# Attention outputs left in their own layout, with packed softmax sums, in a macaron block

## The chip, the cores and the metric

One core of one Trainium2 chip runs the whole program. The metric is device time of one execution in microseconds (us); the kernel before took 467.0 us in the median of three runs (466.22 to 468.55).

## The reference

The block works on x of shape (4, 256, 512), 4 batches of 256 tokens:

```python
x = x + 0.5 * ffn(layernorm(x))      # 16 experts, 2 of them per token, and a shared expert
x = x + attention(layernorm(x))
x = x + 0.5 * ffn(layernorm(x))      # same weights

# attention: 32 heads of 16 columns, one k and one v for all heads
scores = einsum('bqhd,bkd->bhqk', q, k) * 0.25 + alibi      # causal mask
attn = einsum('bhqk,bkd->bqhd', softmax(scores), v).reshape(B, S, 512)
return attn @ Wo
```

The change touches the attention from the softmax's sums on, and the two places where an FFN hands over.

## The kernel before

Tokens lie in 8 tiles of 128 (two per batch). The program has three stages: `ffn_*(0)`, `att_*`, `ffn_*(1)`. Each engine runs its own list of instructions in the order of the program; semaphores (`wait_ge`, `then_inc`) are the only ties between them. No planner is involved: the order is written out by hand. SP issues nearly all DMAs, in order too, so a wait in `att_sp` holds back every DMA behind it.

**The attention loop.** It runs over the 4 batches b, and in each over 8 rounds q of 4 heads (n = 8b + q, 32 rounds in all). In one round PE does, in this order, with the names that the text uses:

- S0, S1, S2, S3: `scores(b + 1, h, bank)`, the scores of four heads of the **next** batch, queries on partitions (L1551 to L1553). They only serve to find each row's maximum. They use two PSUM banks in turn, so S2 waits until VectorE has read S0.
- T0, T1: `scores_t(b, g)`, the scores of two heads each of **this** batch, keys on partitions (L1565, L1567), between the S. They wait for ScalarE's exponentials of two T before.
- W: `weigh(n - 1)` at the round's end (L1579): the probabilities of the round before times `vv`, which holds 16 columns of v and a column of ones, so that each head's 32 rows of the product are 16 outputs, the softmax's sum, and zeros. It writes bank PS_O.
- between S1 and S2, `turn_back(n - 2)` (L1589): two transposes that bring W's result, copied by ScalarE to `oT`, back to tokens on partitions, in bank PS_A.

The order is S0 T0 S1 turn_back S2 T1 S3 W. In batch 3 there is no next batch and so no S.

VectorE runs `maxima` (L1159) for each S, here M0 to M3, and between M1 and M2 `normalise(n - 2)` (L1187, L1189): reciprocal of 8 sums, and a product of 128x128. ScalarE runs two exponentials (`exps`, L762) and one copy (`outputs`, L743) a round. GpSimd zeroes what the mask hides (`later_zero`).

Some rounds have more. Round 4 and round 0 have `maxima_signed`, `max_turn` (PE) and `maxima_parts` (four small VectorE steps), which split the maxima into bf16 parts, that SP's `m_rows` takes over DRAM to `qside`; since `max_turn` uses PS_A, the next `turn_back` waits for `m_parts`. In rounds 2 and 3 of the next batch `attn_turn` (L1601) turns the normalised outputs again, 4 transposes for each tile, and ScalarE copies them (`turned`, L747). In rounds 5 and 6 `out_product` (L1607) multiplies them by Wo, a tile each, and VectorE adds them to x (`residual`, L1195). Round 7 ends with `row_stats` and `ln_stats` for the second FFN. Behind the last round come `xn_turn` for the second FFN and the turns and products of batch 3.

**The hand-over from the first FFN.** `ffn_sp` loads the experts' rows of each tile (`y_rows`) into `yg`, 512 KB each: tiles 0 to 3 first, tiles 4 to 7 once `shared_up` is over (they overwrite `xnT`). VectorE's `pairs_x(t)` (L1014, L1016) adds them to x. `shared_h(7)` (L856) gives `shared_down(6)` and `shared_down(7)` on PE (L1358) what they wait for; behind `shared_down(6)`, PE goes on to `xa_turn(0, ...)` (L1511).

Of the kernel before, what the change touches and what calls it, by code (L numbers as in the profile page):

```python
# [111 lines left out]
def build(nc, x_in, wqkv_in, wo_in, rw_in, rb_in, rbias_in, ew1, eb1, ew2, eb2, ew3, eb3,  # L112
          sw1, sb1, sw2, sb2, sw3, sb3, const_f, const_b, rows_q, rows_k, out):
    with ExitStack() as ctx:
# [14 lines left out]
        k_dram = nc.dram_tensor("k_dram", (BATCH, HD, len(KPART), SEQ), BF16).ap()  # L129
        m_dram = nc.dram_tensor("m_dram", (2, 3, QT * HEADS, P), BF16).ap()  # L130
# [116 lines left out]
        aT_at = used["att"]  # L247
        aT0 = view("att", [P, KC, P])
        oT = view("att", [P, SEQ])
        rec = view("att", [P, QT, 4])  # L250
# [4 lines left out]
        vv = view("att", [P, BATCH, QT, 32])  # L255
        kp = view("att", [HD, 3, SEQ], BF16, at=aT_at)
        kvT = view("att", [2 * HD, SEQ])
        used["att"] = max(used["att"], early)
        attn = [view("att", [P, QT, DIM]) for _ in range(2)]
        xa = attn[::-1]  # L260
        xaT0 = view("att", [P, KC, SEQ])
        aT = (aT0, xaT0.rearrange("p c t -> p (c t)")[:, 0:KC * P].rearrange("p (c q) -> p c q", c=KC))
# [49 lines left out]
        def at_bank(b, t):  # L312
            return PS_O if b + 1 == BATCH and t == 1 else PS_A
# [13 lines left out]
        def ffn_sp(f):  # L327
# [32 lines left out]

            nc.sync.wait_ge(sem("s_gu"), NT * f + NT)
            y_rows(range(4, NT))
            if f == 0:
                nc.sync.wait_ge(sem("s_z"), NT)
                nc.sync.dma_start(wo, wo_in.rearrange("(c p) n -> p c n", p=P)).then_inc(sem("wo_in"), 16)

        def att_sp():
# [186 lines left out]
        def att_pool():  # L554
# [39 lines left out]
            for b in range(BATCH):  # L594
                for q in range(HEADS // 4):
                    later_zero(8 * b + q)
                    if q == 1 and b >= 2:
                        ln_rstd(1, b - 2)
# [112 lines left out]
        def att_act():  # L711
# [26 lines left out]
            def outputs(n):  # L738

                act.wait_ge(sem("pv"), n + 1)  # L740
                if n >= 1:
                    act.wait_ge(sem("ot"), n)
                act.copy(oT[:], ps[:, PS_O, 0:SEQ]).then_inc(sem("oT"), 1)  # L743

            def turned(b, t):
                act.wait_ge(sem("a_at"), QT * b + t + 1)
                act.copy(aT[t].rearrange("p c q -> p (c q)"), ps[:, at_bank(b, t), :]).then_inc(sem("a_aT"), 1)  # L747
# [998 lines left out]
```

## Time and profile before

| | |
|---|---|
| median of 3 runs | 467.0 us |
| the profiled execution | 467.78 us |
| its span, first to last instruction | 466.0 us |
| clock granted to TensorE, mean | 0.97 |
| busy in the span | PE 409.6 us (88%), VectorE 261.9 (56%), ScalarE 180.3 (39%), GpSimd 162.7 (35%) |

By stretch, from the view of busy time in windows:

| stretch, us | what | PE busy | VectorE busy | ScalarE busy |
|---|---|---|---|---|
| 121 to 201 | end of FFN 0, projections | 67.92 of 80 | 54.05 | 15.18 |
| 201 to 231 | loop, batch 0 | 28.41 of 30 | 24.12 | 17.10 |
| 231 to 265 | loop, batch 1 | 31.39 of 34 | 23.81 | 16.41 |
| 265 to 298 | loop, batch 2 | 32.06 of 33 | 22.88 | 16.31 |
| 298 to 327 | loop, batch 3 | 24.48 of 29 | 12.97 | 16.79 |
| 441 to 466 | last sums, output | 14.13 of 25 | 14.57 | 0.95 |

Matmuls overlap in the pipeline and their ends are modelled: a matmul of the table can take part of the next one's time, so the start of one to the start of the next is the better measure. Times in the text are from the start of the span. "Idle before" names the one that came last of those that the instruction waited for.

### The profile page before, as it was taken

What the parts mean: (1) busy time and instruction counts of PE and PEld (TensorE: products, weight loads), DVE (VectorE), ACT (ScalarE), POOL (GpSimd) and SP (SyncE); (2) the same over time, 40 slices, a digit from 0 to 9 for tenths busy, and PEclk for the clock granted to TensorE, in tenths of its full rate; (3) what the DMA queues carried; (4) which work ended last, traced back from release to release, by engine and by line L of the source; (5) the groups of instructions that cost most, each with busy time, mean ns of one, the idle gap of its engine ahead of it and who ended that gap; (6) DMA issues with size and microseconds to landing.
All of it is one profiled execution on the core that took longest, in us unless ns stands there. A gap on an engine that the chain in (4) does not pass through costs nothing.

```text
span 466.0 us, 8466 instructions
## 1 busy us (share of the span) xinstructions
PE 409.6 (88%) x2848; PEld 289.0 (62%) x2849; DVE 261.9 (56%) x729; ACT 180.3 (39%) x300; POOL 162.7 (35%) x230
## 2 busy tenths in 40 slices
PE   0799879999959979879999899798999879999982
PEld 1687567888636757546665465343687558888650
DVE  5489513333258955868885785633239932333347
ACT  1321235665102221146663364483522316665300
POOL 2611316665302852333332242252000054666300
PEclk9999998999979999979999999999999989999987
DMA  7999973534296479212211200020120042444277
GB/s 213 312 372 313 322 234 129 171 108 158 99 364 191 129 181 194 75 39 73 74 56 26 69 6 6 0 74 24 46 91 1 1 134 79 171 132 147 95 269 305
DMA packets 48620, 63.88 MB, mean 137 GB/s; under 512 B 7750, under 2 KB 28070, under 8 KB 48548
## 3 DMA queue, kind: packets, MB, share of 16 engines
q1 hardware_dynamic: 40220, 41.51, 28.2%
q0 software_dynamic: 6368, 19.19, 12.8%
q10 hardware_dynamic: 2000, 2.76, 2.0%
q8 instruction: 19, 0.31, 0.3%
q14 instruction: 13, 0.11, 0.1%
HBM read 46.06 MB, written 19.79 MB: 141 GB/s over the span
## 4 chain that ended last, share of the span: by engine, by line
PE 57%; DVE 15%; DMA 9%; SPq 9%; issue 5%; POOL 2%; ACT 1%; ACTq 0%; POOLq 0%; DVEq 0%
PE ps L1453 14%; PE ps L1460 7%; PE ps L1607 6%; SPq L320 5%; PE ps L1579 5%; PE ps L1438 3%; DMA w<-in_L_ffn_ew_dram 3%; PE ps L1317 3%; PE ps L1522 3%; PE ps L1551 3%; DMA q_dram<-arena 2%; DVE arena L1159 2%; PE ps L1553 2%; PE ps L1565 2%; PE ps L1589 2%
## 5 line engine op out<-in xcount | busy, mean ns | idle before, releaser
L1159 DVE TENSOR_REDUCE arena<-ps 128x3 f32<-128x384 f32 x128 | 67.2, 550 | 17.5 <-PE ps L1553 16.7
L1453 PE MATMUL ps<-arena,wj 128*128 128x128 f32 x608 | 75.5, 278 | 0.0
L1453 PEld LDWEIGHTS ps<-arena,wj 128*128 128x128 f32 x608 | 72.6, 195 | 1.0 <-issue 1.0
L762 ACT ACTIVATE arena<-ps 128x768 f32<-128x768 f32 x64 | 51.8, 811 | 50.7 <-PE ps L1567 49.8
L592 POOL TENSOR_SCALAR_AFFINE_SELECT arena<-arena 128x512 f32<-128x512 f32 x64 | 40.8, 637 | 83.3 <-ACT arena L762 82.9
L1056 DVE SCALAR_TENSOR_TENSOR arena<-ps,arena 128x128 f32<-128x128 f32 x38 | 13.3, 351 | 87.6 <-ACT arena L678 87.6
L1317 PE MATMUL ps<-arena,turns 128*128 128x256 f32 x256 | 57.6, 381 | 0.0
L1317 PEld LDWEIGHTS ps<-arena,turns 128*128 128x128 f32 x256 | 48.2, 190 | 8.1 <-issue 2.1
L524 POOL DMA_INDIRECT y_dram<-arena x38 | 38.4, 1011 | 40.1 <-DVE arena L1063 31.6
L519 POOL DMA_INDIRECT arena<-xn_dram,arena x34 | 33.2, 977 | 51.4 <-DVE arena L996 25.2
L1460 PE MATMUL ps<-w,arena 128*128 x76 | 40.1, 611 | 4.0 <-DVE arena L1056 4.0
L1551 PE MATMUL ps<-cb 128*128 128x256 bf16 x128 | 36.1, 282 | 5.0 <-DVE arena L1159 4.5
L1358 PE MATMUL ps<-turns,arena 128*128 128x512 f32 x64 | 33.7, 653 | 7.1 <-issue 7.1
L683 ACT COPY wj<-w 128x1024 f32 x38 | 39.6, 1047 | 0.0
L1553 PE MATMUL ps<-arena 116*128 116x256 bf16 x128 | 35.5, 278 | 0.0
L674 ACT COPY arena<-ps 128x512 f32<-128x512 f32 x38 | 22.3, 587 | 31.4 <-PE ps L1438 31.4
L1522 PE MATMUL ps<-arena,wj 128*128 128x256 f32 x128 | 31.6, 383 | 1.5 <-ACT arena L720 1.5
L632 ACT ACTIVATE arena<-ps,shb 128x256 f32<-128x256 f32 x16 | 7.6, 473 | 59.3 <-PE ps L1317 59.3
L1438 PEld LDWEIGHTS ps<-cf,arena 128*128 128x128 f32 x136 | 17.3, 145 | 20.3 <-issue 18.5
L1607 PE MATMUL ps<-turns,arena 128*128 128x512 f32 x64 | 29.5, 604 | 0.0
L1552 PE MATMUL ps<-arena 116*128 116x128 bf16 x128 | 28.8, 225 | 0.0
L1579 PE MATMUL ps<-arena 128*32 128x128 f32 (+1 forms) x512 | 27.8, 335 | 0.0
(190 smaller groups left out, 609.7 us busy)
## 6 DMA issues: line engine op xcount, KB each, us to landing
arena<-y_dram SPq DMA_DIRECT2D x16, 512.0 KB, 7.4
arena<-q_dram SPq DMA_DIRECT2D x36, 128.0 KB, 2.6
xn_dram<-arena SPq DMA_DIRECT2D x16, 256.0 KB, 5.8
w<-in_L_ffn_ew_dram SPq DMA_DIRECT2D x4, 1024.0 KB, 10.9
q_dram<-arena SPq DMA_DIRECT2D x16, 192.0 KB, 2.4
x<-_attn_hidden_states_dram SPq DMA_DIRECT2D x4, 512.0 KB, 6.0
out_dram<-x SPq DMA_DIRECT2D x8, 256.0 KB, 4.7
turns<-in_L_ffn_sw_dram ACTq DMA_DIRECT2D x3, 512.0 KB, 7.8
```

Of the source, the lines that this page charges most:

```text
L592: pool.affine_select(diagonal, diagonal, [[0, 2], [0, 2], [1, P]], ALU.is_ge, 0.0, base=0, channel_multiplier=-1).then_inc(sem("sel"), 1)
L683: act.copy(wj[:, par].rearrange("p c f -> p (c f)"), w12[:, ds(e, 1)].rearrange("p a c f -> p (a c f)")).then_inc(sem(f"wj{f}"), 1)
L762: act.activation(pr[:, n % 2, pair, :], ps[:, bank:bank + 2, :].rearrange("p a b -> p (a b)")[:, 0:768], ACT.Exp).then_inc(sem("exp"), 1)
L1159: dve.tensor_reduce(m3[:, h:h + 1, :], ps[:, bank, 0:3 * P].rearrange("p (n k) -> p n k", n=3), AX_X, ALU.max).then_inc(sem("s_max"), 1)
L1317: ins = pe.matmul(o, sw12[:, c, cols], xnT[:, 2 * pair:2 * pair + 2, c, :], start=(c == 0), stop=(c == KC - 1))
L1453: ins = pe.matmul(o, wj[:, par, c, n * INTER:(n + 1) * INTER], xgT[:, par, c, :], start=(c == 0), stop=(c == KC - 1))
L1460: pe.matmul(ps[:, PS_Y + par, :], hj[:, par, :], w3[:, ds(e, 1), :], start=True, stop=True).then_inc(sem(f"y{f}"), 1)
L1522: ins = pe.matmul(ps[:, PS_ST + c, 0:SEQ], wq[:, k, c * P:(c + 1) * P], xaT[b % 2][:, k, :], start=(k == 0), stop=(k == KC - 1))
L1551: pe.matmul(o.rearrange("p (n k) -> p n k", k=P)[:, 0:3:2, :], identb, mask, start=True, stop=True)
L1553: pe.matmul(o[:, P:3 * P], qside[0:R_MAX, p, h, P:2 * P], kT[0:R_MAX, b, :], start=False, stop=True, skip_group_check=True).then_inc(sem(" ...
L1579: ins = pe.matmul(o, vv[:, b, k, :], pr_blocks(n % 2, h // 2)[:, k * QT:(k + 1) * QT - k, h % 2, :], start=(k == 0), stop=True, skip_group ...
L1607: ins = pe.matmul(ps[:, at_bank(b, t), :], aT[t][:, c, :], wo[:, c, :], start=(c == 0), stop=(c == KC - 1))
```

## The change

Outputs stay with heads on partitions. `vv` becomes v and ones in alternate columns, 34 wide; a round with even n takes columns 1 to 32 (outputs in even rows, sums in odd rows), one with odd n takes columns 0 to 31 (the reverse). ScalarE copies an even round's result to `aT[b % 2][:, c, :]`, an odd round's to `odd`; a pair of rounds p (16 pairs) fills one of 4 chunks c of `aT`. SP then issues three DMAs a pair: the even rounds' sums and the odd rounds' sums into `sums` (4 rows for each head group, packed for a whole batch; in batch 3 a full tile for each chunk), and the odd rows of `odd` into `aT`. Once a batch, VectorE takes one reciprocal of `sums`, 128x256; SP writes it to `r_dram` and reads it back with 8 DMAs that repeat each row over 16 partitions; VectorE multiplies `aT`, 128x1024. `turn_back`, `attn_turn` and `turned` go. `out_product` becomes `out_part`, four pieces a tile, spread over rounds. Further, `max_turn(0, 1)` moves into the loop, `residual` and `row_stats` move, `y_rows` of tiles 4 to 6 waits for less, and `shared_h(7)` moves ahead of `pairs_x(1)`. Wo is loaded in two DMAs with its rows interleaved to match. The diff, cut:

```diff
         def at_bank(b, t):
-            return PS_O if b + 1 == BATCH and t == 1 else PS_A
+            return PS_S + 1 - t if b + 2 == BATCH else PS_O if b + 1 == BATCH and t == 1 else PS_A
...
+            nc.sync.wait_ge(sem("s_gu"), NT * f + NT - 2)
+            y_rows(range(4, NT - 1))
             nc.sync.wait_ge(sem("s_gu"), NT * f + NT)
-            y_rows(range(4, NT))
+            y_rows((NT - 1,))
...
+            def sums_of_even(p):
+                sp.wait_ge(sem("oT"), 2 * p + 1)
+                if last and c >= 2:
+                    sp.wait_ge(sem("normed"), b + c - 1)
...
+                sp.dma_start(into[rows], aT[b % 2][rows.start + 1::rows.step, c]).then_inc(sem(f"even_sums{p % 2}"), 16)
+
+            def odd_in(p):
+                sp.wait_ge(sem("oT"), 2 * p + 2)
...
+                sp.dma_start(into[rows.start + 1::rows.step], odd[rows]).then_inc(sem(f"odd_in{p % 2}"), 16)
+                sp.wait_ge(sem(f"even_sums{p % 2}"), 16 * (p // 2 + 1))
+                sp.dma_start(aT[b % 2][1::2, c], odd[1::2]).then_inc(sem(f"odd_in{p % 2}"), 16)
+
+            def inverses(b):
+                sp.wait_ge(sem("a_rec"), b + 1)
+                if b >= 1:
+                    sp.wait_ge(sem("normed"), b)
+                sp.dma_start(r_dram, sums[b % 2]).then_inc(sem("r_out"), 16)
+                sp.wait_ge(sem("r_out"), 16 * (b + 1))
+                for h in range(4):
+                    for g in range(2):
+                        at = 32 * h + g
+                        sp.dma_start(inverse[at:32 * h + 32:2], r_dram[at:at + 2 * KC:2].partition_broadcast(HD)).then_inc(sem("r_in"), 16)
+
             for b in range(BATCH):
+                sums_of_even(4 * b)
+                odd_in(4 * b)
+                if b >= 1:
+                    inverses(b - 1)
+                sums_of_even(4 * b + 1)
                 if b + 2 < BATCH:
                     q_rows(b + 2, 0, HEADS // 2)
+                odd_in(4 * b + 1)
                 if b + 1 < BATCH:
                     m_rows(b + 1, 0)
+                sums_of_even(4 * b + 2)
+                odd_in(4 * b + 2)
+                sums_of_even(4 * b + 3)
                 if b + 2 < BATCH:
                     q_rows(b + 2, HEADS // 2, HEADS)
+                odd_in(4 * b + 3)
                 if b + 1 < BATCH:
                     m_rows(b + 1, 1)
...
+                if n % 2 == 0:
+                    act.copy(aT[b % 2][:, c, :], ps[:, PS_O, 0:SEQ]).then_inc(sem("oT"), 1)
+                else:
+                    if p >= 1:
+                        act.wait_ge(sem(f"odd_in{(p - 1) % 2}"), 32 * ((p - 1) // 2 + 1))
+                    act.copy(odd[:], ps[:, PS_O, 0:SEQ]).then_inc(sem("oT"), 1)
...
+            def invert(b):
+                for par in range(2):
+                    dve.wait_ge(sem(f"even_sums{par}"), 32 * (b + 1))
+                    dve.wait_ge(sem(f"odd_in{par}"), 64 * (b + 1))
+                dve.reciprocal(sums[b % 2], sums[b % 2]).then_inc(sem("a_rec"), 1)
+
+            def normalise(b):
+                dve.wait_ge(sem("r_in"), 16 * 8 * (b + 1))
+                dve.tensor_tensor(aT[b % 2], aT[b % 2], inverse, ALU.mult).then_inc(sem("normed"), 1)
+
+            def normalise_last(c):
...
+                dve.reciprocal(s, s).then_inc(sem("a_rec"), 1)
+                dve.wait_ge(sem("a_rec"), b + c + 1)
+                dve.tensor_tensor(aT[b % 2][:, c, :], aT[b % 2][:, c, :], s, ALU.mult).then_inc(sem("normed"), 1)
...
             pairs_x(0)
+            shared_h(7)
             pairs_x(1)
             att_stats(0)
-            shared_h(7)
...
                     if more:
                         maxima(b + 1, 4 * q, PS_S)
                         maxima(b + 1, 4 * q + 1, PS_S + 1)
-                    if n >= 2:
-                        normalise(n - 2)
+                    if q == 2 and b >= 1:
+                        invert(b - 1)
+                    if q == 4 and not more:
+                        normalise(b - 1)
+                    if q in (4, 6) and not more:
+                        normalise_last(q // 2 - 2)
+                    if q == 6 and b >= 1:
+                        residual(b - 1, 0)
+                    if q == 0 and b >= 2:
+                        residual(b - 2, 1)
                     if more:
                         maxima(b + 1, 4 * q + 2, PS_S)
                         maxima(b + 1, 4 * q + 3, PS_S + 1)
...
+                    if q == 4 and b >= 1 and more:
+                        normalise(b - 1)
                     if q == 7 and b >= 1:
-                        row_stats(b - 1)
+                        row_stats(QT * (b - 1))
+                    if q == 1 and b >= 2:
+                        row_stats(QT * (b - 2) + 1)
+                        ln_stats(1, b - 2)
...
-                        turn_back(n - 2)
+                    if q == 5 and b >= 1 and more:
+                        pe.wait_ge(sem("m_parts"), 2 * b + 3)
+                        out_part(b - 1, 0, 0)
+                        out_part(b - 1, 0, 1)
...
+                    if b >= 1 and more:
+                        if q == 5:
+                            out_part(b - 1, 0, 2)
+                            out_part(b - 1, 0, 3)
+                        if q == 6:
+                            pe.wait_ge(sem("att_x"), QT * (b - 1) + 1)
+                        if q >= 6:
+                            out_part(b - 1, 1, 2 * q - 12)
+                            out_part(b - 1, 1, 2 * q - 11)
+                    if not more:
+                        if q in (5, 6):
+                            for c in range(KC):
+                                out_part(b - 1, q - 5, c)
+                        if q == 7:
+                            pe.wait_ge(sem("m_parts"), 2 * b + 2)
+                            out_part(b, 0, 0)
...
+            out_part(BATCH - 1, 0, 1)
+            for c in range(KC - 2):
+                out_part(BATCH - 1, 1, c)
+            for t in range(QT):
+                out_part(BATCH - 1, t, KC - 2)
             xn_turn(1, 4)
-            out_product(BATCH - 1, 0)
             xn_turn(1, 5)
-            out_product(BATCH - 1, 1)
+            for t in range(QT):
+                out_part(BATCH - 1, t, KC - 1)
```

## Rows read from the trace of the kernel before

**Rows 1.** Chain that ended last; columns: start, us, what.

```profile
131.25 4.75 issue
```

**Rows 2.** PE and VectorE in one plain quarter of batch 0.

```profile
209.59 0.28 PE L1551 MATMUL ps<-cb 128*128 128x256 bf16 x1
...
210.08 1.16 DVE L1159 TENSOR_REDUCE arena<-ps 128x3 f32<-128x384 f32 x2 [0.95 <-PE ps L1553]
...
210.48 0.38 PE L1589 MATMUL ps<-cf,arena 128*128 128x128 f32 x2
...
210.70 0.27 PE L1551 MATMUL ps<-cb 128*128 128x256 bf16 x1
...
212.47 0.28 PE L1551 MATMUL ps<-cb 128*128 128x256 bf16 x1
```

**Rows 3.** PE and its weight loads late in batch 1.

```profile
260.15 0.10 PEld L1551 LDWEIGHTS ps<-cb 128*128 128x128 bf16 x1 [0.26 <-DVE arena L1159]
...
264.94 0.28 PE L1551 MATMUL ps<-cb 128*128 128x256 bf16 x1 [1.73 <-DVE arena L1159]
```

**Rows 4.** ScalarE by line and shape: busy us, mean ns.

```profile
L762 ACT ACTIVATE arena<-ps 128x768 f32<-128x768 f32 x64 | 51.8, 811 | 50.7 <-PE ps L1567 49.8
...
L743 ACT COPY arena<-ps 128x256 f32<-128x256 f32 x32 | 11.9, 372 | 7.4 <-PE ps L1579 7.4
```

**Rows 5.** VectorE in order of time: start, us, work, [idle before <-releaser].

```profile
135.41 0.48 DVE L856 SCALAR_TENSOR_TENSOR arena<-ps,shb,arena 128x256 f32<-128x256 f32 x1
...
140.22 0.69 DVE L1004 SCALAR_TENSOR_TENSOR x<-ps,x 128x512 f32<-128x512 f32 x1 [2.87 <-PE ps L1362]
```

**Rows 6.** PE at the loop head; stretch with PEclk 0.50.

```profile
201.23 0.27 PE L1595 MATMUL ps<-cf,arena 128*64 128x128 f32 x1 [2.12 <-DVE arena L1168]
...
203.00:204.00 1.00, 0.77 (x4) 0.54 (x5) 0.65 (x3) 0.16 (x1) 0.65 (x1) 0.50 0.08 12
```

**Rows 7.** PE: starts of weigh (L1579), and one turn_back (L1589).

```profile
220.07 0.44 PE L1589 MATMUL ps<-cf,arena 128*128 128x128 f32 x2 [0.38 <-DVE arena L1180]
...
237.15 0.86 PE L1579 MATMUL ps<-arena 128*32 128x256 f32 x16
...
243.89 0.86 PE L1579 MATMUL ps<-arena 128*32 128x256 f32 x16
...
265.93 0.86 PE L1579 MATMUL ps<-arena 128*32 128x256 f32 x16
...
279.37 0.86 PE L1579 MATMUL ps<-arena 128*32 128x256 f32 x16
...
298.66 0.86 PE L1579 MATMUL ps<-arena 128*32 128x256 f32 x16
```

**Rows 8.** VectorE by line and shape: busy us, mean ns.

```profile
L896 DVE RECIPROCAL arena<-arena 128x8 f32<-128x8 f32 x2 | 0.4, 205 | 0.1
...
L959 DVE TENSOR_TENSOR arena<-arena 128x8 f32<-128x8 f32 x2 | 0.3, 162 | 0.0
...
L1016 DVE SCALAR_TENSOR_TENSOR x<-arena,hv,x 128x512 f32<-128x512 f32 x16 | 12.1, 756 | 0.6
```

**Rows 9.** DMA issues: tiles, queue, count, KB, median us to landing.

```profile
arena<-y_dram SPq DMA_DIRECT2D x16, 512.0 KB, 7.4
...
arena<-q_dram SPq DMA_DIRECT2D x36, 128.0 KB, 2.6
...
m_dram<-arena SPq DMA_DIRECT2D x16, 12.0 KB, 1.5
```

**Rows 10.** SP's queue: us that its instructions took to issue.

```profile
202.74 0.80 SPq L403 DMA_DIRECT2D m_dram<-arena  x2
...
227.16 3.82 SPq L389 DMA_DIRECT2D arena<-q_dram  x6
```

**Rows 11.** PE in the last batch and behind it.

```profile
313.64 3.70 PE L1607 MATMUL ps<-turns,arena 128*128 128x512 f32 x8
...
338.35 5.34 PE L1317 MATMUL ps<-arena,turns 128*128 128x256 f32 x24
```

More of the change, by code:

```diff
@@ L246, in build @@
         kT = view("att", [P, BATCH, SEQ], BF16)
[L247 to L250, printed above, removed]
+        kp_at = used["att"]
+        kp = view("att", [HD, 3, SEQ], BF16)
+        odd = view("att", [P, SEQ])
         m3 = view("att", [P, HEADS, 3])
@@ L784, in att_act @@
                 xnT_copy(1, t)
-            for t in range(QT):
-                turned(BATCH - 1, t)
             xnT_copy(1, 4)
@@ L1595, in max_turn, with out_part @@
                 pe.transpose(ps[0:QT * HEADS, m_bank(b, half), 0:P], nm[:].rearrange("p t h -> p (t h)"), ident).then_inc(sem("m_t"), 1)
-            def attn_turn(b, t):
-                pe.wait_ge(sem("normed"), 8 * (b + 1))
-                for c in range(KC):
-                    ins = pe.transpose(ps[:, at_bank(b, t), c * P:(c + 1) * P], attn[b % 2][:, t, c * P:(c + 1) * P], ident)
-                ins.then_inc(sem("a_at"), 1)
-            def out_product(b, t):
-                pe.wait_ge(sem("a_aT"), QT * b + t + 1)
-                for c in range(KC):
-                    ins = pe.matmul(ps[:, at_bank(b, t), :], aT[t][:, c, :], wo[:, c, :], start=(c == 0), stop=(c == KC - 1))
-                ins.then_inc(sem("a_wo"), 1)
+            def out_part(b, t, c):
+                pe.wait_ge(sem("normed"), b + 1 if b + 1 < BATCH else b + c + 1)
+                ins = pe.matmul(ps[:, at_bank(b, t), :], aT[b % 2][:, c, t * P:(t + 1) * P], wo[:, c, :], start=(c == 0), stop=(c == KC - 1))
+                if c == KC - 1:
+                    ins.then_inc(sem("a_wo"), 1)
             def first_scores(heads):
@@ L1695, in att_pe @@
+                    if not more:
+                        if q == 5:
+                            pe.wait_ge(sem("s_max"), HEADS * BATCH)
+                        if q in (5, 6):
[4 more added lines that the diff above has]
+                            out_part(b, 0, 0)
             last = 8 * BATCH - 1
-            turn_back(last - 1)
+            pe.wait_ge(sem("att_x"), QT * (BATCH - 1))
@@ L1697, in att_pe @@
             xn_turn(1, 0)
             weigh(last)
-            xn_turn(1, 1)
-            turn_back(last)
-            xn_turn(1, 2)
-            xn_turn(1, 3)
-            attn_turn(BATCH - 1, 0)
-            pe.wait_ge(sem("oT"), last + 1)
-            attn_turn(BATCH - 1, 1)
+            for t in range(1, 4):
+                xn_turn(1, t)
+            pe.wait_ge(sem("oT"), last + 1)
+            out_part(BATCH - 1, 0, 1)
+            for c in range(KC - 2):
+                out_part(BATCH - 1, 1, c)
```

124 lines of the change are left out of this document (49 added, 75 removed).

## The prediction, made before the changed kernel was run

> **What bounds the kernel now.** I read the stretches first: PE is busy nearly throughout the loop, so the next question is whether its work or its waits set a round's length. The chain of waits names the entry to attention: PE stands for 4.75 us from 131.25 [rows 1]. The timeline of one plain round then gives the answer for the loop [rows 2]. S0 starts at 209.59, VectorE's M0 at 210.08 (0.49 later), turn_back at 210.48, S2 at 210.70, the next S0 at 212.47: a round is 2.88 us. The reader should see two clocks that meet at S2. PE's own: turn_back costs 210.70 - 210.48 = 0.22. VectorE's: S2 needs the bank that M0 reads, M0 takes 0.55 of the 1.16 for M0 and M1, and 210.08 + 0.55 + 0.07 is 210.70 as well. Where turn_back ended earlier, the weight load of S2 shows a wait for VectorE of 0.26 right behind it [rows 3]. So turn_back fills a gap that PE has anyway. In batch 3 there is no S, and ScalarE paces a round: 2 x 0.811 + 0.372 = 2.0 us [rows 4].
>
> **The change part by part.** The sum is made against the profiled execution, 467.78 us (its span of 466.0 and 1.78 around it), which lies 0.78 above the median of the runs.
>
> *Entry to attention, -2.7.* PE stands until shared_h(7), done at 135.41 + 0.48 [rows 5], behind pairs_x(1) and att_stats(0) in VectorE's list. Ahead of them it can start once its silu is there, about 131.8, and shared_down(6) starts at 132.4 instead of 136.0. The next thing on PE, xa_turn, needs att_norm(0), whose time doesn't move (about 137.0, since all else ahead of it stays); before it started at 140.0. VectorE's own stall of 2.87 for shared_down(6) [rows 5] goes. What follows is a chain of engines and DMAs, all started from there, so I let the shift through: 3.0 at full clock. PE still stands from about 134.3 to 137.0, so part of it may run at the lower clock: bounds -1.4 and -3.2. The earlier y_rows puts tiles 4 to 6 behind tiles 0 to 3 in the same queue: 0, at best -0.5; were seven tiles served side by side, the first four would come later, up to +2. The Trainium skill, "DMA: Bandwidth & Descriptors", section "Queues, rings and completion order", says that each DMA engine consumes one queue's descriptors in ring order; by that rule it is 0, and otherwise up to +2.
>
> *Head of the loop, -0.6.* max_turn(0, 1) held PE for 2.12 us [rows 6]; in the loop S0, T0 and S1 run ahead of it, and S2 follows M0 at about 201.7, 1.5 before its old time. maxima_parts then delays M0 of round 1 by 0.9. Bounds 0 and -3.6, the latter if the lower clock behind that wait (0.50 granted [rows 6]) goes too.
>
> *turn_back, 0.* 22 of the 32 lie beside M0 as above. Bounds 0 and 22 x -0.22 = -4.8. Its wait for m_parts (0.38 [rows 7]) is free too: M0 of that round queues behind the same maxima_parts, so S2 is as late. In batch 3 it is ScalarE's pace.
>
> *attn_turn, -2.0.* Rounds 2 to 4 of batch 1, with two of them, took 243.89 - 237.15 = 6.74 [rows 7], so each costs (6.74 - 2 x 2.88) / 2 = 0.49. Four in batches 1 and 2. The signed maxima lose 0.2 of this cover a batch: +0.4.
>
> *invert, +2.1.* The trace has a reciprocal of 8 columns only, 205 ns beside 162 for a product of 8 [rows 8]. If the extra 43 is paid per column, 5.4 + 1.0 a column, 256 columns take 1.8 us; if once, 0.46. I take 1.8, as a longer latency alone would show in other deep instructions too. It stands between M1 and M2, where normalise took 0.44 with no slack left; M2 is late, and so is the next S0: +1.05 in batches 1 and 2. Bounds 0 and +2.6. 
>
> *The inverses' way and normalise, with the product in pieces, -1.1 for batch 1 and +0.7 for batch 2.* Count from the start of W in round 2. ScalarE's copy is done at 1.2; SP issues odd_in's two DMAs until 2.1. Then r_dram: landing 2.1 (between 1.5 for 12 KB and 2.6 for 128 KB [rows 9]). Then 8 issues. One costs 0.40 where rows are few, 0.64 for q_rows [rows 10]; I take 0.42, near the former, as 64 rows each are nearer to its 48. Landing 2.4. Sum: 2.1 + 2.1 + 7 x 0.42 + 2.4 = 9.6. VectorE comes to normalise at 9.15 (round 4's W at 7.0, M3, maxima_parts), and multiplies 1024 columns for 1.25 (twice 0.756 for 512, less one start [rows 8]): 10.9. PE, at S1's end since 8.9, stands 1.95, then does two pieces (1.8), and M0 and M1 lie hidden. W of round 5 starts at 13.7, 3.1 behind where a round with parts puts it, for 1.8 of work. After that each of rounds 5 to 7 carries two pieces, 2.88 + 1.81, and the stall of 1.73 at the end of round 7 [rows 3] goes, because row_stats is halved and hides under the pieces. From W of round 4 to W of the next round 0: 6.8 + 3 x 4.69 = 20.9 against 265.93 - 243.89 = 22.04 [rows 7]: -1.1. In batch 2 the old end was cheap: 298.66 - 279.37 = 19.29 [rows 7] against 19.4, +0.1; and row_stats with ln_stats in round 1 delays M0 by 0.6. Bounds for both batches by the inverses' landing: normalise never waits (-0.9), or the 512 KB take 7.4 like y_rows' 512 KB [rows 9] behind the last issue (+10).
>
> *SP's queue, 0.* Batch 1 is the fullest: 12 small DMAs x 0.4, 9 of inverses x 0.42, 13 of q_rows and k_rows x 0.64, 8 of m_rows x 0.35, and waits for landings of some 4, so 24 of about 36 us. The first place where a late SP would reach PE is ScalarE's copy to `odd`, which waits for the pair before; by my clock odd_in(5) lands at 15, the copy wants it at 18. For this and the 0.4 us of more waiting, bounds 0 and +3.
>
> *Batch 3 and the tail, -1.2.* Before, W of round 0 started at 298.66 [rows 7], the first out_product at 313.64, and the last ended at 338.35 [rows 11]. Rounds 0 to 4 now run at ScalarE's 2.05, so PE would be at the product at 11.0 behind W of round 0. But its inverses: SP is at them at 6.1, they land at 13.6, normalise ends at 14.9: PE starts the product where it did, at 15.0, after standing for 3.8. All that the missing turns give in rounds 0 to 4 is eaten. From there: product 3.63, T0 and T1 0.7, W 0.79, product 3.63, T0 and T1 0.7, to W of round 7 at 24.4 (before 26.2); W of the last at 26.5; then xn_turn 1.3, three pieces 2.7, two 1.8, xn_turn 0.9, two 1.8: 36.0 against 338.35 - 298.66 = 39.7. normalise_last(3), with two DMAs and 1.8 + 0.4 on VectorE, is done at about 33, ahead of PE at 34.2. So -3.7. Against it, PE has stood for 3.8 us, and at both waits of over 2 us in these rows the granted clock was 0.50 right after it (4.75, 2.12) while it stayed full after 1.73: I add 2.5 for some 5 us at 1.2 instead of 2.4 GHz. Bounds -4.5 and +2.
>
> Sum: -2.7 - 0.6 - 2.0 + 0.4 + 2.1 - 1.1 + 0.7 - 1.2 = -4.4, so 463.4 us, 0.8% below 467.0.
>
> **The rivals.**
> - *PE's sum binds.* Every removed transpose is gained: 32 x 0.22 + 8 x 0.49 = 11.0, entry and head as above 3.3: 453.5. For it, PE's busy share; against it, the wait behind turn_back [rows 3].
> - *The way of the inverses is short.* Issues at 0.3, the reciprocal's extra paid once, no fall of the clock in batch 3: 463.4 - 2.1 - 0.9 - 2.5 = 457.9.
> - *Two more falls of the clock.* PE's wait of 1.95 in round 5 lies between 1.73 and 2.12. If it grows a little, batches 1 and 2 lose 2.5 to 3 each: 469.0.
> - *The inverses come late (the other side).* One mechanism: eight broadcasts of 512 KB over DRAM, in SP's in-order queue, land after VectorE is at normalise, which stands ahead of M0; each us of it is a us of PE, three times. The profile gives 7.4 for 512 KB by one kind of DMA. Break-even is at 1.5 us more than my 9.6. At 2.0 to 2.5 more in each batch, with the clock falling in batches 1 and 2 too: 463.4 + 6.6 + 5 = 475.
>
> **How the numbers follow.** My forecast has 0.42 (its own range 461 to 466.5), PE's sum 0.07, the short way 0.20, two more falls 0.11, late inverses 0.20. Within 0.5% of 467.0, which is about what a measurement of this kernel can tell from no change, means 464.7 to 469.3: faster is 0.30 of my forecast and both faster rivals, 0.57; same is 0.12 of it and the falls, 0.23; slower 0.20. The range from 456.5 to 471.5 leaves out PE's sum and most of the late inverses.
>
> **What would show it.** Right: a plain round still takes 2.88 us with an idle gap of 0.2 before S2 named VectorE; the reciprocal of 256 columns near 1.8 us; normalise (1.25) ended by a DMA wait in round 4 of batches 1 to 3; PE idle about 2, 2 and 4 us ahead of the first piece, and a clock of 0.50 behind the last of them; shared_down(6) near 132.4. Wrong: rounds of 2.66 us; no DMA wait ahead of normalise; a ScalarE copy that waits for a DMA; a loop entry that is not some 3 us earlier.

## The result, and the profile after

The changed kernel took 472.2 us in the median of 4 runs (471.1 to 473.69), the kernel before 466.6 beside it. The ratio is 1.011 with the interval 1.0072 to 1.0149: slower, where I had forecast 463.4. Ratios here and below come from the fast executions run side by side and medians from all, so the two can differ by a little. The profiled execution took 472.57 us, its span 470.8. First the page's busy times and its clock line (40 equal slices, the granted clock in tenths):

```profile
PE 401.1 (85%) x2752; PEld 277.5 (59%) x2753; DVE 265.4 (56%) x678; ACT 174.2 (37%) x292; POOL 163.4 (35%) x230
...
PEclk9999998999999999899997998995999989999998
```

TensorE works 8.5 us less than before (401.1 for 409.6) and the kernel is slower all the same, so what grew is waiting. Its waits, by what it waited for (us in total, times, longest):

```profile
PE ps L1658 <- DVE arena L1236: 16.4, 3, 7.0
PE ps L1618 <- DVE arena L1203: 11.2, 14, 2.1
...
PE ps L1632 <- DMA arena<-m_dram: 1.5, 1, 1.5
```

L1658 is `out_part`, L1236 `normalise`. Three waits, one a batch, make 16.4 us; I had forecast 1.95 + 1.95 + 3.8 = 7.7. The 1.5 for `m_dram`, once in batch 3, is new too; all kernels below with packed sums have a wait there, from 0.6 (order alone) to 1.8 (four broadcasts). TensorE in order of time, the same three places:

```profile
247.24 3.75 PE L1658 MATMUL ps<-turns,arena 128*128 128x512 f32 x4 [4.70 <-DVE arena L1236]
...
287.11 3.46 PE L1658 MATMUL ps<-turns,arena 128*128 128x512 f32 x4 [4.75 <-DVE arena L1236]
...
322.87 6.07 PE L1658 MATMUL ps<-turns,arena 128*128 128x512 f32 x8 [6.96 <-DVE arena L1236]
```

Each wait costs twice. Without a fall of the clock four of these matmuls take 1.95 us and eight 3.70 (below, in the kernel without the way over DRAM; eight took 3.70 before too [rows 11]). Here they take 3.75, 3.46 and 6.07. Stretches of 2 us, with PEclk behind the five busy times:

```profile
246.00:248.00 2.00, 0.76 (x1) 0.50 (x2) 2.00 (x3) 0.00 (x0) 0.00 (x0) 0.50 0.65 195
...
250.00:252.00 2.00, 2.00 (x8) 0.84 (x7) 0.44 (x1) 0.00 (x0) 0.00 (x0) 0.50 0.27 70
...
288.00:290.00 2.00, 2.00 (x4) 0.82 (x3) 0.00 (x0) 0.00 (x0) 0.00 (x0) 0.50 0.07 15
...
325.00:327.00 2.00, 2.00 (x3) 0.73 (x3) 2.00 (x3) 0.00 (x0) 0.00 (x0) 0.50 0.10 33
```

Why VectorE is late stands in its own rows: the reciprocal, then `normalise`, which waits for a DMA.

```profile
233.26 1.75 DVE L1231 RECIPROCAL arena<-arena 128x256 f32<-128x256 f32 x1 [0.50 <-DMA arena<-arena]
...
245.87 1.23 DVE L1236 TENSOR_TENSOR arena<-arena 128x1024 f32<-128x1024 f32 x1 [3.00 <-DMA arena<-r_dram]
```

And why the DMA is late stands in SP's queue: start, us of issuing, tiles. L433 is `sums_of_even`, L441 and L443 `odd_in`, L450 the store to `r_dram`, L455 the eight broadcasts. First batch 1, then batch 3.

```profile
234.19 0.51 SPq L433 DMA_DIRECT2D arena<-arena  x1
234.74 0.59 SPq L441 DMA_DIRECT2D arena<-arena  x1
236.41 0.47 SPq L443 DMA_DIRECT2D arena<-arena  x1
236.92 0.59 SPq L450 DMA_DIRECT2D r_dram<-arena  x1
238.88 5.09 SPq L455 DMA_DIRECT2D arena<-r_dram  x8
...
309.69 0.58 SPq L409 DMA_DIRECT2D arena<-m_dram  x2
...
312.25 0.47 SPq L443 DMA_DIRECT2D arena<-arena  x1
312.82 0.53 SPq L450 DMA_DIRECT2D r_dram<-arena  x1
314.71 5.13 SPq L455 DMA_DIRECT2D arena<-r_dram  x8
```

In batch 1 W of round 2 starts at 233.20. The store goes out 3.7 behind it (forecast 2.1), because `odd_in`'s second DMA waited for the even heads' sums until 236.41 and a small DMA takes 0.5 to 0.6 to issue, where I used 0.4. Those sums had gone out late themselves, at 234.19, 2.6 behind ScalarE's copy (done at 231.61), as `m_rows` held SP until then. The store lands 1.96 later (forecast 2.1). The eight broadcasts take 0.64 each to issue (forecast 0.42), and the last lands at 245.87, 7.0 behind the first issue (forecast 5.3). Sum 12.7 behind W where I had 9.6. In batch 2 the store goes out 2.5 behind W, near the forecast, and the inverses still land 12.0 behind it: there the eight broadcasts take 5.88 to issue, and the last lands 7.6 behind the first issue. In batch 3 W of round 0 starts at 304.11. Here `m_rows` holds SP with its landings, the store goes out 8.7 behind W (forecast 6.1), and the inverses land 17.4 behind it (forecast 13.6).

The places where the change gains, TensorE at the entry and at the first rounds, and one between them where it loses:

```profile
133.33 1.96 PE L1425 MATMUL ps<-turns,arena 128*128 128x512 f32 x4 [1.13 <-issue]
...
138.02 1.07 PE L1578 MATMUL ps<-cf,arena 128*128 128x128 f32 x8 [2.52 <-DVE arena L1175]
...
185.68 0.28 PE L1618 MATMUL ps<-cb 128*128 128x256 bf16 x1 [2.06 <-DVE arena L1203]
...
205.19 0.86 PE L1646 MATMUL ps<-arena 128*32 128x256 f32 x16
...
208.07 0.86 PE L1646 MATMUL ps<-arena 128*32 128x256 f32 x16
```

W of round 1 starts at 205.19, before at 208.46, 3.3 earlier. From there to the end of the last piece of the output product (346.59) it is 141.4 us, before 130.1; behind it 124.2, before 127.5. So the span's +4.8 is -3.3 + 11.3 - 3.3 (rounded). I had forecast -3.3 - 1.1 + 0 for these. The last -3.3 I could not tie to the change: in executions of this study the stretch behind the product lasted from 124 to 130 us, in kernels that have nearly the same code there. Part of it is the clock: behind the product it was below full for some 14 us before (379 to 384, 451 to 455, 461 to 466) and for some 7 in the changed kernel (382 to 386, 467 to 470).

### The profile page after: what moved, and what is told of

Its sections match the earlier page's. It is cut to its first block, busy times and chain, and to the rows that moved or that the text cites. A ratio compares the mean times of both kernels' runs of the same rounds, so it can differ in the third digit from the quotient of the medians.

```text
span 470.8 us, 8251 instructions
## 1 busy us (share of the span) xinstructions
PE 401.1 (85%) x2752; PEld 277.5 (59%) x2753; DVE 265.4 (56%) x678; ACT 174.2 (37%) x292; POOL 163.4 (35%) x230
## 3 DMA queue, kind: packets, MB, share of 16 engines
q0 software_dynamic: 6368, 19.19, 12.6%
## 4 chain that ended last, share of the span: by engine, by line
PE 50%; DVE 16%; SPq 14%; DMA 11%; issue 5%; POOL 2%; ACT 1%; ACTq 0%; DVEq 0%; POOLq 0%
PE ps L1520 14%; PE ps L1658 7%; PE ps L1527 7%; SPq L320 5%; PE ps L1384 4%; PE ps L1505 3%; DMA w<-in_L_ffn_ew_dram 3%; PE ps L1646 3%; SPq L455 3%; DVE arena L1203 3%; PE ps L1618 2%; DMA q_dram<-arena 2%; PE ps L1425 2%; PE ps L1620 2%; SPq L343 2%
## 5 line engine op out<-in xcount | busy, mean ns | idle before, releaser
L1203 DVE TENSOR_REDUCE arena<-ps 128x3 f32<-128x384 f32 x128 | 68.7, 553 | 33.3 <-PE ps L1620 31.0
L1658 PE MATMUL ps<-turns,arena 128*128 128x512 f32 x64 | 36.4, 706 | 16.4 <-DVE arena L1236 16.4
L1425 PE MATMUL ps<-turns,arena 128*128 128x512 f32 x64 | 31.8, 621 | 3.5 <-issue 3.5
L1589 PE MATMUL ps<-arena,wj 128*128 128x256 f32 x128 | 31.6, 383 | 1.5 <-ACT arena L765 1.5
L1618 PEld LDWEIGHTS ps<-cb 128*128 128x128 bf16 x128 | 12.6, 98 | 33.2 <-DVE arena L1203 22.9
L1658 PEld LDWEIGHTS ps<-turns,arena 128*128 128x128 f32 x64 | 13.0, 222 | 30.3 <-issue 30.3
```

Of the source, the lines that this page charges most:

```text
L1203: dve.tensor_reduce(m3[:, h:h + 1, :], ps[:, bank, 0:3 * P].rearrange("p (n k) -> p n k", n=3), AX_X, ALU.max).then_inc(sem("s_max"), 1)
L1425: ins = pe.matmul(ps[:, z_bank(t), :], hidden[t // 2 % 2][:, c, t % 2 * P:(t % 2 + 1) * P], sw3s[:, c, :], start=(c == 0), stop=(c == SHAR ...
L1618: pe.matmul(o.rearrange("p (n k) -> p n k", k=P)[:, 0:3:2, :], identb, mask, start=True, stop=True)
L1658: ins = pe.matmul(ps[:, at_bank(b, t), :], aT[b % 2][:, c, t * P:(t + 1) * P], wo[:, c, :], start=(c == 0), stop=(c == KC - 1))
```

## The experiments

Ratios are to the kernel before, run beside each group. One profiled execution can lie some us off its kernel's median: "short reciprocals" (478.54) 5.9 above, "later pieces" (466.13) 3.2, "order alone" (470.73) 2.5 and "four broadcasts" (470.38) 2.2 above, "four, and order" (457.19) 5.7 below. The last column, from these executions, is to be read with that in mind. "Loop" is the profiled stretch from W of round 1 to the end of the output product.

| kernel | median us | before beside it | ratio, 95% | loop us |
|---|---|---|---|---|
| changed | 472.20 | 466.61 | 1.0072 to 1.0149 | 141.4 |
| two broadcasts | 477.01 | 467.09 | 1.0114 to 1.0236 | 145.3 |
| short reciprocals | 472.61 | 467.09 | 1.0051 to 1.0113 | 144.0 |
| y_rows as before | 471.35 | 467.09 | 1.0056 to 1.0114 | 139.1 |
| moves alone | 463.33 | 467.09 | 0.9846 to 0.9946 | 129.7 |
| four broadcasts | 468.18 | 468.25 | 0.9925 to 0.9999 | 133.2 |
| four, and order | 462.88 | 468.25 | 0.9835 to 0.9931 | 127.1 |
| order alone | 468.28 | 468.25 | 0.9952 to 1.0025 | 135.3 |
| ready inverses | 456.35 | 468.25 | 0.9681 to 0.9789 | 121.6 |
| later pieces | 462.96 | 469.67 | 0.9784 to 0.9885 | 128.8 |
| pieces behind W | 465.29 | 469.67 | 0.9865 to 0.9935 | 129.1 |

My theory was that the way of the inverses over SP and DRAM makes the stall; the first rival that VectorE's packed work does; the second that the transfer does, and not its issue.

**Two broadcasts.**

```diff
-                for h in range(4):
-                    for g in range(2):
-                        at = 32 * h + g
-                        sp.dma_start(inverse[at:32 * h + 32:2], r_dram[at:at + 2 * KC:2].partition_broadcast(HD)).then_inc(sem("r_in"), 16)
+                for g in range(2):
+                    rows = r_dram[g].rearrange("(h m) t -> h (m t)", h=4)[:, None, 0:KC * SEQ]
+                    sp.dma_start(inverse[g::2].rearrange("p c t -> p (c t)"), rows.to_broadcast([4, HD, KC * SEQ])).then_inc(sem("r_in"), 16)
```

`r_dram`'s layout and the count that `normalise` waits for change with it.

> The changed kernel, but r_dram is laid out so that 2 DMAs instead of 8 bring the inverses of a batch back (256 KB each, rows of 4 KB). Theory A, the inverses' way through SP's queue sets the loss: 6 issues of 0.65 us less are 3.9 us less on the way, the waits ahead of normalise of 3.0, 3.05 and 10.4 us fall to about 0, 0 and 6.5, PE's idle time ahead of the first pieces from 16.4 to about 6.5, and the two falls of the clock in batches 1 and 2 go: 456 to 460 us. Rival B, VectorE's own new work (reciprocals of 1.75 us and products of 1.2 us) sets it: no change, 471 to 473. Rival C, the bytes set it and not the issues: two DMAs of 256 KB land some 5 us after issue, so the way is as long as before and the time 469 to 472.

Slower still, 1.0175: rival C's mechanism, at more than its price. The chain of waits (start, us, what) has the landing of these transfers in it three times:

```profile
238.14 8.33 DMA arena<-r_dram
...
278.75 7.09 DMA arena<-r_dram
...
315.87 6.78 DMA arena<-r_dram
```

The issue fell to 1.2 us, but 256 KB whose outermost dimension has 4 entries took 6.8 to 8.3 us to land. So fewer DMAs did not help in this shape. The Trainium skill, "DMA: Bandwidth & Descriptors", section "Why a DMA increments its semaphore by 16 and not by 1", says that a copy is dealt to the largest number of DMA engines, up to 16, that divides the slowest dimension of both its sides: four here, 16 in the changed kernel's copies, whose repeat of 16 is outermost. The durations fit that rule, and so does the share of the 16 engines that was busy (the number behind the granted clock, then GB/s). Here are two stretches of 2 us of this kernel in batch 2, and one of "four, and order" below in batch 3:

```profile
281.00:283.00 2.00, 1.10 (x9) 0.69 (x9) 1.07 (x4) 1.19 (x2) 0.68 (x2) 1.00 0.26 104
283.00:285.00 2.00, 0.00 (x0) 0.00 (x0) 0.00 (x0) 0.00 (x0) 0.44 (x1) 1.00 0.26 104
...
302.00:304.00 2.00, 0.01 (x1) 0.00 (x0) 0.00 (x0) 0.00 (x0) 0.16 (x1) 1.00 0.83 210
```

0.26 of 16 is about four engines. The share is a mean; no row here shows the engines singly.

**Short reciprocals.** All seven reciprocals work on 8 of 256 columns.

```diff
-                dve.reciprocal(sums[b % 2], sums[b % 2]).then_inc(sem("a_rec"), 1)
+                dve.reciprocal(sums[b % 2][:, 0:8], sums[b % 2][:, 0:8]).then_inc(sem("a_rec"), 1)
...
-                dve.reciprocal(s, s).then_inc(sem("a_rec"), 1)
+                dve.reciprocal(s[:, 0:8], s[:, 0:8]).then_inc(sem("a_rec"), 1)
```

> The changed kernel with each of its 7 reciprocals over 8 of 256 columns only, the other sums left uninverted. Theory A: a_rec comes 1.55 us earlier, but SP comes to r_dram later than that anyway, and VectorE then waits at normalise for as much longer: the stall of PE behind invert in batches 1 and 2 goes (about 1.1 each), the wait at normalise grows by the same: 471 to 472.5, no change. Rival B: 7 x 1.55 us, or at least the 5 that stand in PE's way, go: 461 to 465.

The same time as the changed kernel, as theory A has it. VectorE in batch 1, in an execution 5.9 above the median:

```profile
234.52 0.20 DVE L1231 RECIPROCAL arena<-arena 128x8 f32<-128x8 f32 x1 [1.00 <-DMA arena<-arena]
...
246.61 1.22 DVE L1236 TENSOR_TENSOR arena<-arena 128x1024 f32<-128x1024 f32 x1 [4.01 <-DMA arena<-r_dram]
```

TensorE's wait behind the reciprocal fell from 1.43 to 0.39, and VectorE's wait for `r_dram` grew from 3.00 to 4.01: what the reciprocals save is waited for later. VectorE's own work is not the bound.

**y_rows as before.**

```diff
-            nc.sync.wait_ge(sem("s_gu"), NT * f + NT - 2)
-            y_rows(range(4, NT - 1))
             nc.sync.wait_ge(sem("s_gu"), NT * f + NT)
-            y_rows((NT - 1,))
+            y_rows(range(4, NT))
```

> The changed kernel with the transfers of y_rows for tiles 4 to 7 waiting for shared_up(7) again, as before the change, in both FFNs. My prediction had 0 for this edit. The trace now shows VectorE without its wait of 1.59 us for tile 2 in the last sums. If the early issue is the cause, this kernel is 1.5 to 2 us slower than the changed one (474), with the wait for tile 2 back; if not, it is within 0.5 us of it. At the entry to attention it makes no difference, as nothing there waits for tiles 4 to 6.

Its interval covers the changed kernel's ratio of 1.011: the early `y_rows` is worth nothing that the times can show, as forecast. Its trace has a second wait of VectorE for `y_rows` back in the last sums (0.98 us at 457.10; the changed kernel has one wait there, the kernel before two), so the edit may give about 1 us, too little for these runs to tell.

**Moves alone.** The kernel before, with `shared_h(7)` ahead of `pairs_x(1)`, the early `y_rows`, and `max_turn(0, 1)` with its maxima in the loop; outputs turned and normalised as before.

```diff
+            shared_h(7)
             pairs_x(1)
...
-            shared_h(7)
...
-            maxima_signed(0, 1)
-            maxima_parts(0, 1)
...
-            max_turn(0, 1)
```

> The kernel before with only the moves: shared_h(7) ahead of pairs_x(1), maxima_signed(0,1), max_turn(0,1) and maxima_parts(0,1) inside the loop, and y_rows of tiles 4 to 6 early. Outputs are turned and normalised as before. Theory A says that all that the changed kernel gained before the first inverses comes from these: entry -3.0, head of the loop with its low clock -1 to -1.5, last sums 0 to -1.6. So 461 to 463 against 466.6 for before. A rival, that the gain at W of round 1 (3.3 us in the trace) comes from the new weighing and copies, would leave it at 465 to 467.

0.9896, faster. W of round 1, and the next:

```profile
203.86 0.86 PE L1579 MATMUL ps<-arena 128*32 128x256 f32 x16
...
206.73 0.86 PE L1579 MATMUL ps<-arena 128*32 128x256 f32 x16
```

That is 4.6 earlier than before, and its loop of 129.7 us is that of before (130.1), 12 shorter than the changed kernel's. So the moves give a gain by themselves, and the rest of the change costs about 2% (1.011 against 0.9896).

**Four broadcasts.** `r_dram` holds even and odd rows apart, so that one DMA fills 32 partitions and its outermost dimension is the 16 repeats.

```diff
+                rows = r_dram.rearrange("g (h m) t -> h g (m t)", h=4)[:, None, :, 0:KC * SEQ]
                 for h in range(4):
-                    for g in range(2):
-                        at = 32 * h + g
-                        sp.dma_start(inverse[at:32 * h + 32:2], r_dram[at:at + 2 * KC:2].partition_broadcast(HD)).then_inc(sem("r_in"), 16)
+                    sp.dma_start(inverse[32 * h:32 * h + 32].rearrange("p c t -> p (c t)"),
+                                 rows[h].to_broadcast([HD, 2, KC * SEQ])).then_inc(sem("r_in"), 16)
```

> Changed: the inverses of a batch come back from DRAM in four transfers of 128 KB, each to 32 partitions, with rows of 4 KB, where the changed kernel has eight of 64 KB. Theory A (the way of the inverses over SyncE sets the stall ahead of the output product's first pieces, and eight issues of 0.64 us are most of it): four issues in about 2.6 us where eight took 5.1 to 5.9, so the inverses land 2 to 3 us earlier in each of the three batches, TensorE's wait ahead of the first piece goes from 4.7, 4.75 and 7.0 us to about 2, 2 and 4.5, the clock falls perhaps one time less, and the time is 463 to 468. Theory C (what counts is the transfer and not its issue, as in the run with two broadcasts): a transfer of twice the bytes takes twice the time, the inverses land no earlier, 471 to 474.

0.9962: 1.5% off the changed kernel, as theory A has it. TensorE at the first pieces of batches 1 to 3:

```profile
249.10 1.10 PE L1658 MATMUL ps<-turns,arena 128*128 128x512 f32 x2 [1.61 <-DVE arena L1236]
...
284.42 3.46 PE L1658 MATMUL ps<-turns,arena 128*128 128x512 f32 x4 [2.82 <-DVE arena L1236]
...
318.69 5.10 PE L1658 MATMUL ps<-turns,arena 128*128 128x512 f32 x8 [4.36 <-DVE arena L1236]
```

Waits of 8.8 us in sum for 16.4. From the reciprocal's start to `normalise` it is 10.8 for 12.6 us in batch 1, where VectorE no longer waited for the inverses (in batch 3 it still did, 8.48).

**Order alone**, with the eight broadcasts.

```diff
                 sums_of_even(4 * b)
-                odd_in(4 * b)
                 if b >= 1:
                     inverses(b - 1)
+                odd_in(4 * b)
```

> Changed: only SyncE's order (the inverses of a batch ahead of the copies of the odd heads of the next batch's round 1), with the changed kernel's eight transfers. Theory A: the inverses land 2 to 3 us earlier per batch, 465 to 469. Theory D: ScalarE's copy of the outputs waits for the odd heads' buffer, which SyncE frees 6 us later, and the time is 470 to 475.

0.9988, on theory A's side. But theory D shows too, in batch 3, where rounds are short:

```profile
245.98 3.48 PE L1658 MATMUL ps<-turns,arena 128*128 128x512 f32 x4 [2.42 <-DVE arena L1236]
...
283.52 3.48 PE L1658 MATMUL ps<-turns,arena 128*128 128x512 f32 x4 [3.36 <-DVE arena L1236]
...
317.00 1.51 PE L1646 MATMUL ps<-arena 128*32 128x256 f32 x16 [6.40 <-ACT arena L795]
```

The wait for the product is gone there, and a wait of 6.40 for ScalarE's copy to `odd` is new.

**Four, and order.** Both edits above. Its profiled execution is the fastest of its six.

> Changed: the four transfers of the run with four broadcasts, and on SyncE the inverses of a batch are sent out ahead of the copies of the odd heads (odd_in) of the next batch's round 1, where the changed kernel sends them behind these. Theory A: the store no longer stands behind odd_in's wait and its two issues (3.7 us behind the reciprocals' start in batch 1), so with the shorter issue the inverses land 4.5 to 6 us earlier than in the changed kernel; TensorE's wait ahead of the first pieces goes to 0 to 1 us in batches 1 and 2 and to 2 to 3 us in batch 3, two or three of the falls of the clock go, and the time is 455 to 460. Theory D (the stall moves to what is now behind SyncE: odd_in comes 4 us later, its odd heads' buffer is handed on late and ScalarE's next output copy waits): the rounds behind the inverses stretch by 2 to 4 us and the time stays at 466 to 472.

0.9883, faster than before and 2.2% faster than the changed kernel, but not the 455 to 460 of theory A. Its six runs went from 457.19 (the profiled one, mean clock 0.986) to 464.83 (0.966). SP's queue in batch 1:

```profile
232.55 0.57 SPq L450 DMA_DIRECT2D r_dram<-arena  x1
234.66 2.52 SPq L454 DMA_DIRECT2D arena<-r_dram  x4
```

VectorE there:

```profile
230.77 1.75 DVE L1231 RECIPROCAL arena<-arena 128x256 f32<-128x256 f32 x1 [0.74 <-DMA arena<-arena]
...
240.29 1.21 DVE L1236 TENSOR_TENSOR arena<-arena 128x1024 f32<-128x1024 f32 x1
```

ScalarE in batch 3:

```profile
305.34 0.37 ACT L795 COPY arena<-ps 128x256 f32<-128x256 f32 x1 [3.89 <-DMA arena<-arena]
```

TensorE in batch 1 and in batch 3:

```profile
241.65 1.95 PE L1658 MATMUL ps<-turns,arena 128*128 128x512 f32 x4 [1.61 <-DVE arena L1236]
...
305.86 1.51 PE L1646 MATMUL ps<-arena 128*32 128x256 f32 x16 [3.85 <-ACT arena L795]
```

In batches 1 and 2 `normalise` has no DMA wait any more: 9.52 us from the reciprocal is VectorE's own time (with 0.46 of waiting for `max_turn`), and the way is hidden. Four matmuls take 1.95. In batch 3 the wait stays, as one of 3.85 for the copy to `odd`; `normalise` ended at 306.17 there, so without it TensorE would have stood at the pieces nearly as long.

**Ready inverses.** No store, no broadcasts, so `inverse` is never filled; `normalise` waits for the reciprocals alone; every other instruction stays. The edit, cut:

```diff
-                dve.wait_ge(sem("r_in"), 16 * 8 * (b + 1))
+                dve.wait_ge(sem("a_rec"), b + 1)
                 dve.tensor_tensor(aT[b % 2], aT[b % 2], inverse, ALU.mult).then_inc(sem("normed"), 1)
```

> Changed: the way over DRAM is left out altogether; normalise waits for the reciprocals alone and multiplies by a buffer that is not filled anew (the outputs of batches 0 to 2 are therefore scaled by other numbers), with every other instruction in place. Theory A (the way of the inverses costs all that the change loses): no wait ahead of the first pieces beyond VectorE's own work, no fall of the clock there, 452 to 458, which is 5 to 11 us below the run that had the moves alone (463.3) when the sums packed into one reciprocal are worth their forecast. Theory B (the loss is in VectorE's packed work, the pieces in TensorE's queue or the turned order, not in the way): 465 to 472, no better than the changed kernel.

0.9735, in theory A's range. TensorE at the first pieces of batches 1 and 3:

```profile
244.83 1.95 PE L1650 MATMUL ps<-turns,arena 128*128 128x512 f32 x4 [1.61 <-DVE arena L1228]
...
306.07 3.70 PE L1650 MATMUL ps<-turns,arena 128*128 128x512 f32 x8
```

The stretch behind the first of these waits, with its clock at 1.00:

```profile
246.00:248.00 2.00, 2.00 (x18) 1.03 (x20) 0.85 (x2) 0.58 (x1) 0.00 (x0) 1.00 0.18 51
```

The loop takes 121.6 us, 8.1 less than with the moves alone and 19.8 less than in the changed kernel. Of the 19.8, waits ahead of the pieces make 16.4 - 3.2 = 13.2, the slow matmuls (3.75 - 1.95) + (3.46 - 1.95) + (6.07 - 3.70) = 5.7, which leaves 0.9. This kernel takes away the way and the time that it holds SP's queue together; "four broadcasts" and "order alone" show that each is part of it.

**Later pieces**, on top of "four, and order": in batch 3 `odd_in` goes first again, and TensorE's eight pieces stand a quarter later.

```diff
+                if b + 1 == BATCH:
+                    odd_in(4 * b)
                 if b >= 1:
                     inverses(b - 1)
-                odd_in(4 * b)
+                if b + 1 < BATCH:
+                    odd_in(4 * b)
...
-                        if q in (5, 6):
+                        if q in (6, 7):
                             for c in range(KC):
-                                out_part(b - 1, q - 5, c)
+                                out_part(b - 1, q - 6, c)
```

> Changed against the run with four broadcasts and the new order: in the last batch only, SyncE takes the copies of the odd heads of round 1 first and then the inverses, and TensorE's eight output pieces of the batch before stand one quarter later (behind quarters 6 and 7 instead of 5 and 6). In that run's trace TensorE waited 3.85 us for the odd heads' copy on ScalarE (305.86) with the store of the inverses ahead of it, and the clock fell behind that wait. Theory A (a stall goes where the way over DRAM runs beside rounds that do not need it): ScalarE no longer waits for the odd heads' buffer, the inverses land about 2.3 us later but the rounds of quarters 4 and 5 run in front of the pieces, TensorE waits under 1.5 us in all, no fall of the clock, and the time is 454 to 459. Theory D (the wait only moves: to the pieces, or to the residual and the last batch's sums behind them): 461 to 466, like that run.

0.9834 (0.986 by the medians), no better than the kernel it is built on within the intervals. Theory D: the wait moved back to the pieces.

```profile
302.72 0.38 PE L1635 MATMUL ps<-arena 119*128 119x512 bf16 x1 [1.29 <-DMA arena<-m_dram]
...
312.26 1.22 PE L1661 MATMUL ps<-turns,arena 128*128 128x512 f32 x1 [4.14 <-DVE arena L1239]
```

**Pieces behind W**, on top of it: in batches 1 and 2 the first two pieces stand behind W of round 4 with the other two, and no longer ahead of S2.

```diff
-                    if q == 5 and b >= 1 and more:
-                        pe.wait_ge(sem("m_parts"), 2 * b + 3)
-                        out_part(b - 1, 0, 0)
-                        out_part(b - 1, 0, 1)
...
                         if q == 5:
+                            pe.wait_ge(sem("m_parts"), 2 * b + 3)
+                            out_part(b - 1, 0, 0)
+                            out_part(b - 1, 0, 1)
```

> Changed against the run with later pieces: in batches 1 and 2 all four pieces of query tile 0 stand behind the outputs of quarter 5, where two of them stood ahead of its second pair of scores. TensorE waited 1.6 us for VectorE's normalise at the first of them in each batch, in that run and in the one without any way over DRAM. Theory A (the wait is an order of the queue: the scores and outputs behind it were ready): 1.5 us fewer per batch, 2 to 3 us off the time of the run with later pieces, 451 to 457. Theory B (VectorE is the bound around the reciprocals of 1.75 us and the product of 1.2 us; the scores' banks come free only by its maxima): TensorE waits as long at the scores instead, and the time is the same within 1 us.

0.99, not faster: theory B for the wait, though not for its "same within 1 us" (the median is 2.3 higher, with overlapping intervals). TensorE now stands at S2 in that place, longer than it stood at the piece (1.61):

```profile
245.42 0.40 PE L1621 MATMUL ps<-cb 128*128 128x256 bf16 x1 [1.99 <-DVE arena L1206]
```

Behind both waits of 1.99 the clock fell (0.50 in 246 to 248 and in 284 to 286); behind those of 1.61 it had stayed at full.

The best kernels of the study that compute the block are "later pieces" and "four, and order", 1.2 to 1.7% faster than before (1.1 to 1.4% by the medians); both beat the changed kernel. Whether they beat the moves alone (0.9896) their intervals don't tell.

## Why the prediction was wrong

- *Entry and loop head, -3.3 together:* the sum came out at W of round 1 in the changed kernel, by luck; it was -4.6 with the moves alone. `xa_turn` started 2.0 earlier (138.02 for 139.97, forecast 3.0), and at the projections TensorE was 3.1 to 3.4 ahead (forecast 2.7), as the clock did not fall at the entry: it waited 2.52 at 138.02 and the stretches behind were at 1.00, where they had been at 0.50 before. Then it waited 2.06 at 185.68, the clock was at 0.50 in 188 to 190, and at 193.60 only 0.65 was left (before, the same matmuls started at 194.25). The loop head gave the other 2.6 (forecast 0.6), as the fall there [rows 6] is gone. In the eight other kernels that have the same code up to there W of round 1 starts at 202.45 to 208.29.
- *turn_back worth nothing:* right. Plain rounds still take 2.88 (208.07 - 205.19), as in [rows 2].
- *invert, 1.8 us:* right in size, 1.75 (paid per column: 8 columns took 0.20), and `normalise` took 1.23 for 1.25. TensorE waited 1.43 and 0.69 behind it in batches 1 and 2, where I had 1.05 each. By the rule that I had cited from the Trainium skill, "VectorE: DVE Perf Modes", section "First, the fixed hardware budget", my estimate was 2.1; the measurement decides for 1.75.
- *attn_turn and the pieces:* the sum without the way held, as far as one trace of each kernel can tell. My forecast of the loop was 130.1 - 1.1 = 129.0; it contained 7.7 of waits and 2.5 of slow clock. Taking these out and putting VectorE's own 3.2 in gives 122.0. The kernel with ready inverses took 121.6.
- *The inverses' way: the step that failed.* "Sum: 2.1 + 2.1 + 7 x 0.42 + 2.4 = 9.6" (9.5 by its terms) was 3.7 + 2.0 + 7.0 = 12.7 in batch 1 and 2.5 + 1.9 + 7.6 = 12.0 in batch 2. I took the issue price of a broadcast from `m_rows`, "as 64 rows each are nearer to its 48", when [rows 10] had 0.64 for another kind; it was 0.64, and 0.73 in batch 2. And I let `odd_in` pass SP without its own wait for the even heads' sums, and without `m_rows` ahead of these in batch 1. In batch 3, 6.1 to the store was 8.7. Waits came to 16.4 for 7.7.
- *One fall of the clock, 2.5:* there were three in the loop, 5.7, and one ahead of it (188 to 190). I had kept batches 1 and 2 just under the waits after which it had fallen, at 1.95; at 4.7 that was over.
- *SP's queue, 0:* no copy of ScalarE waited for a DMA in the changed kernel, as forecast; but the queue set the time all the same, through the inverses themselves.

Against the forecast's 463.4, the profiled 472.57 is +9.2. The waits give +8.7 and the clock +3.2; the stretch behind the product gives -3.3, which I had not forecast, and 0.6 is left; without it the error would have been larger. The rival "the inverses come late" had the mechanism, its place and nearly the price: 2.4 to 3.8 late, 472.2 for its 475 (and 475.5 without the 3.3 behind the product). I gave it 0.20, though my own break-even lay only 1.5 us behind a sum of estimated issues. The run with two broadcasts shows its other half as well, a transfer of 7 to 8 us.

## What to carry to other kernels

Work that is packed to save instructions must come back in time: price the whole way of one packed result, each issue on its queue at the highest price seen for its kind and each wait of the queue ahead of it, and put it against the moment at which the consumer arrives. Where the margin is smaller than the spread of those prices, expect the stall, and add the fall of the clock to it. If the way is issue-bound, fewer and larger DMAs and a place ahead of work that can wait bring more than removing arithmetic; but keep 16 outermost, as the quick transfers here had it, and look where the displaced copy is wanted. And a difference of 2 or 3 us between two traces can be one fall of the clock; look for it before you give it to the change.

## What the runs showed that I had not expected

- The length of TensorE's wait alone does not say whether the clock falls. Behind waits of 1.99 (pieces behind W), 2.12 [rows 6], 2.42 and 3.36 (order alone) it was at or near 0.50; behind 2.52 at the entry of the changed kernel it stayed at 1.00, as it did behind 1.61, 1.73 [rows 3] and 2.07 (pieces behind W, at 315.20). The same wait in the same place did both. All kernels with `shared_h(7)` ahead wait 2.51 or 2.52 at the entry, and the eight matmuls behind it took 1.06 or 1.07 in six of them and 1.54 to 1.94 in the other five, here with ready inverses:

```profile
136.85 1.66 PE L1570 MATMUL ps<-cf,arena 128*128 128x128 f32 x8 [2.52 <-DVE arena L1167]
```

- A broadcast of 256 KB with 4 outermost took 6.8 to 8.3 us to land; four of 128 KB with 16 outermost, issued in 2.52 us, landed within 4.8 us of the first issue (in the kernel with four broadcasts and the new order, batch 3, the first issue was at 300.14 and `normalise` began at 304.94).
- Three times the removal of a stall moved it to a neighbour, at about the same length: to ScalarE's copy (6.40, 3.85), back to the product (4.14), to S2 (1.99).
